# Dispatch of tokens to experts: one buffer region per expert, the first half of the tokens scattered once it is chosen

## Chip, cores and metric

The kernel runs on one core of one Trainium2 chip. The metric is the device time of one execution in microseconds (us); less is better. TensorE is called PE, VectorE DVE, ScalarE ACT, GpSimd POOL and SyncE SP.

## What is computed

The kernel computes a small transformer: x is 4 x 512 x 256 in float32. An attention with 32 query heads and 8 key heads (rotated, causal) is added to x; then a mixture of experts "f"; then a differential attention with 32 heads of 8; then a mixture of experts "h" with the same weights. Norms stand ahead of each. The experts matter here, on 2048 tokens of 256 values:

```python
scores = softmax(xt @ Wg.T)                        # 16 experts
# the best 2 of 4 groups by their largest score, then the best 4 experts of those
topi = top_k(masked, 4)[1]
weights = take_along_axis(scores, topi, axis=1)
h = silu(xt @ W1[e].T) * (xt @ W3[e].T)            # 176 wide, for each expert e
y = sum over the token's 4 experts of weight * (h @ W2[e].T)
z = silu(xt @ Ws1.T) * (xt @ Ws3.T) @ Ws2.T        # shared by all, 352 wide
return y + z
```

## The kernel before

Each engine has its program written out by hand, with semaphores between them. After an attention, `pe_ffn`, `act_seam` and `dve_seam` project its result, add it to x, normalize it into `y_sb` (16 blocks of 128 tokens, with the transposes in `xnT_all`) and compute the scores for 8 blocks at a time (`logits_ps`, half 0 and half 1).

**Choosing.** In `dve_ffn`, `scores(hf)` makes the softmax (ACT does the exponentials) and masks the groups, `choose(hf)` finds the four experts of each token (`pick`, and `taken`, 128 x 8 x 16 of ones and zeros). When both halves are chosen, PE counts (`counts`, L1886): with a triangle of ones and 16 more matmuls it finds each token's rank within its expert over all tokens, and each expert's total. `slots` (L1298) makes of the totals the first row of each expert in `x_slots`, where the experts lie one behind the other, each rounded up to a multiple of `HALF` = 64 rows; `assign(hf)` (L1314) makes the row of each token and choice, `slot_i`. Then `full_tiles`, `pair_units`, `singles`, `places` and `order` work out which rows each of the 72 tiles of 128 rows reads, and which expert it belongs to; they are spread over the steps of the shared experts.

**Shared experts.** PE does `shared_in(k)` and `shared_out(k)` for k = 0 to 11 (3 for each of 4 batches), ACT the silu, DVE the product `hw` and, at every third step, the sum into x (`add_shared`).

**Scatter.** `pool_ffn` writes the tokens into `x_slots` in DRAM, in 64 indirect DMAs (16 blocks x 4 choices, 128 rows of 265 values each): 32 after `assign(0)`, 32 after `assign(1)`. Number n waits for number n - 2, so two are in flight. After the last one come the 80 indirect DMAs that add the results of the tiles to y (`result_out`).

**Tiles.** SP's `sp_ffn_slots` waits for `e_order`, stores x of batches 0 to 2 into y (`store_x`), waits for the first 40 scatters (`EARLY_T` = 10 blocks) and then loads tile after tile from `x_slots` into a ring of 8 (`load(j)`, with the row read from `first_row` into a register), tiles from 24 on only after all 64 scatters. PE turns and multiplies them in pairs; DVE scales result j into `yt`, a ring of 8 too, so that result 8 waits until result 0 has been stored by POOL.

**Clearing.** Rows that no token fills must be zero. In the first attention SP issues after the loads of each of its slots n a clear of 512 rows of `x_slots` (19 in all, L436) and one of y (22, L441). Every fourth slot, SP then moves the maxima `mT` that PE needs (`sp_move_maxima`, L375).

```python
                if s == "a" and n < SLOT_ROWS // (4 * P):
                    sp.dma_start(x_slots[n * 4 * P:(n + 1) * 4 * P, :].rearrange("(a p) e -> p a e", p=P),
                                 zero.unsqueeze(1).to_broadcast([P, 4, EW])).then_inc(sm("cleared"), 16)
```

## Time and profile before

| | |
|---|---|
| median of 3 executions | 1373.87 us (1372.12 to 1375.77) |
| the profiled execution: its time, its span | 1371.78 us, 1370.0 us |
| busy: PE, DVE, ACT, POOL | 1147.9, 874.3, 543.2, 688.1 us |
| DMA: bytes moved, mean rate | 177.42 MB, 129 GB/s |
| mean granted clock of PE | 0.928 |
| first attention, experts f | about 105 to 345 us, 345 to 680 us |
| second attention, experts h | about 780 to 1020 us, 1020 to 1350 us |

Busy times are those in which an engine executes an instruction; a wait is not busy. In rows of the time line a row is start, duration, engine, line of the kernel, operation, out<-in, with in brackets the idle time before it and what ended it. "SPq" rows are the issues of DMAs by SP, "DMA" rows in the chain of waits the transfers themselves.

### The profile page before, as it was taken

The numbers are of one execution on the slowest core, as the hardware profiler recorded it, in microseconds if no ns is written. First come the engines' busy times: TensorE is split into PE (matmuls) and PEld (weight loads), VectorE is DVE, ScalarE is ACT, GpSimd is POOL, SyncE is SP. The second block draws the span as 40 slices with busy tenths as digits, with TensorE's granted clock in tenths as the row PEclk, the third lists the DMA queues.
The fourth block names the chain that finished last, engine by engine and source line by source line (L and its number), as shares of the span: only waits on it lengthen the run. The fifth ranks groups of instructions, "written<-read, shape, count | busy, mean of one in ns | idle before, by whom it ended". The sixth has DMA issues, their size and how long they took to land.

```text
span 1370.0 us, 25841 instructions
## 1 busy us (share of the span) xinstructions
PE 1147.9 (84%) x8690; PEld 616.4 (45%) x8690; DVE 874.3 (64%) x2061; ACT 543.2 (40%) x846; POOL 688.1 (50%) x841
## 2 busy tenths in 40 slices
PE   6888889898889479999568799999888886999990
PEld 2343334342755256665234344444346543665650
DVE  5688889891683135555288799999657722455543
ACT  2124767779421022222122377777855001222210
POOL 4452344444016558777563445555530455777671
PEclk9987999999989799999779899999999997999995
DMA  4424656520913468888664422122044136788868
GB/s 138 145 85 148 187 177 195 156 60 2 297 41 128 133 169 141 150 158 145 105 196 152 152 61 58 52 61 55 10 151 136 64 130 175 151 161 154 156 88 260
DMA packets 154353, 177.42 MB, mean 129 GB/s; under 512 B 20016, under 2 KB 139760, under 8 KB 153712
## 3 DMA queue, kind: packets, MB, share of 16 engines
q1 hardware_dynamic: 124336, 136.38, 34.0%
q0 software_dynamic: 29184, 38.36, 16.4%
q8 instruction: 73, 1.20, 0.4%
q10 hardware_dynamic: 704, 1.02, 0.2%
q14 instruction: 56, 0.46, 0.1%
HBM read 91.12 MB, written 83.78 MB: 128 GB/s over the span
## 4 chain that ended last, share of the span: by engine, by line
PE 49%; DVE 18%; DMA 16%; issue 6%; ACT 5%; SPq 3%; POOL 3%; POOLq 0%; ACTq 0%; DVEq 0%
DMA x_slots<-y_sb,slot_i 11%; PE pair_ps L1976 9%; PE o_ps L1747 8%; DVE nm L1116 4%; ACT arena L842 4%; PE pair_ps L2009 3%; DVE bm L1116 3%; PE pair_ps L2012 2%; PE t_ps L1773 2%; PE pair_ps L1697 2%; PE pair_ps L1578 2%; DMA arena<-mT 2%; PE pair_ps L1672 2%; PE pair_ps L1677 2%; PE pair_ps L1963 2%
## 5 line engine op out<-in xcount | busy, mean ns | idle before, releaser
L842 ACT ACTIVATE arena<-pair_ps 128x1024 f32<-128x1024 f32 x320 | 323.4, 1024 | 133.5 <-PE pair_ps L1672 78.2
L616 POOL TENSOR_SCALAR_AFFINE_SELECT arena<-arena 128x512 f32<-128x512 f32 (+1 forms) x320 | 175.0, 547 | 244.7 <-ACT arena L842 244.2
L1116 DVE TENSOR_REDUCE nm<-pair_ps 128x2 f32<-128x1024 f32 (+1 forms) x192 | 232.5, 1222 | 36.4 <-PE pair_ps L1721 33.2
L685 POOL DMA_INDIRECT x_slots<-y_sb,slot_i x128 | 123.0, 961 | 197.7 <-DVE slot_i L1323 114.1
L1747 PE MATMUL o_ps<-arena 128*9 128x512 f32 (+7 forms) x2048 | 177.3, 441 | 4.2 <-POOL arena L616 4.1
L1976 PE MATMUL pair_ps<-arena 128*128 x512 | 167.8, 469 | 1.8 <-ACT arena L893 1.8
L1116 DVE TENSOR_REDUCE bm<-pair_ps 128x8 f32<-128x1024 f32 x128 | 155.3, 1217 | 4.0 <-PE pair_ps L1721 1.0
L701 POOL DMA_INDIRECT y_f<-xnT,dest x80 | 125.0, 1562 | 42.8 <-DVE xnT L1466 19.3
L701 POOL DMA_INDIRECT y_h<-xnT,dest x80 | 124.6, 1558 | 43.2 <-DVE xnT L1466 20.3
L1449 DVE TENSOR_TENSOR arena<-arena,pair_ps 128x128 f32<-128x128 f32 x144 | 41.4, 288 | 116.2 <-ACT arena L898 74.3
L1976 PEld LDWEIGHTS pair_ps<-arena 128*128 128x128 f32 x512 | 94.2, 195 | 43.4 <-issue 5.9
L898 ACT ACTIVATE arena<-pair_ps 128x176 f32<-128x176 f32 x144 | 45.7, 317 | 145.2 <-PE pair_ps L1976 89.6
L1466 DVE TENSOR_SCALAR xnT<-pair_ps,slot_w 128x256 f32<-128x256 f32 x144 | 64.8, 481 | 55.4 <-PE pair_ps L2014 15.6
L1919 PE MATMUL pair_ps<-arena 128*128 128x512 f32 (+1 forms) x192 | 89.8, 614 | 0.0
L1721 PE MATMUL pair_ps<-c_b 64*128 64x128 bf16 (+1 forms) x1280 | 85.2, 211 | 0.0
L1721 PEld LDWEIGHTS pair_ps<-c_b 64*128 64x128 bf16 x1280 | 60.9, 98 | 34.0 <-issue 4.6
L1672 PE MATMUL pair_ps<-arena 51*128 51x512 bf16 x256 | 51.4, 398 | 21.4 <-DMA arena<-mT 8.5
L893 ACT ACTIVATE arena<-t_ps 128x512 f32<-128x512 f32 x36 | 21.5, 597 | 120.3 <-PE t_ps L1951 90.4
L2009 PE MATMUL pair_ps<-arena 128*128 x224 | 60.4, 393 | 9.4 <-DVE arena L1457 9.4
L1697 PE MATMUL pair_ps<-arena 48*128 48x512 bf16 x256 | 51.4, 395 | 19.2 <-ACT arena L842 14.8
L1747 PEld LDWEIGHTS o_ps<-arena 128*9 128x9 f32 (+1 forms) x2048 | 39.0, 93 | 53.2 <-issue 30.3
L889 ACT ACTIVATE sil<-pair_ps 128x512 f32<-128x512 f32 (+1 forms) x24 | 14.3, 595 | 109.8 <-PE pair_ps L1919 105.2
(273 smaller groups left out, 2019.4 us busy)
## 6 DMA issues: line engine op xcount, KB each, us to landing
arena<-x_slots SPq DMA_DIRECT2D x128, 132.5 KB
arena<-in_w SPq DMA_DIRECT2D x4, 2816.0 KB, 19.0
x_slots<-hw SPq DMA_DIRECT2D x19, 530.0 KB, 3.7
arena<-q_a SPq DMA_DIRECT2D x64, 96.0 KB
arena<-q_b SPq DMA_DIRECT2D x64, 96.0 KB
y_f<-hw SPq DMA_DIRECT2D x11, 512.0 KB, 4.2
y_h<-hw SPq DMA_DIRECT2D x11, 512.0 KB, 4.3
arena<-in_w SPq DMA_DIRECT2D x2, 2048.0 KB, 17.2
```

The source lines that it names most:

```text
L616: pool.affine_select(p, p, pattern, ALU.is_ge, 0.0, base=0, channel_multiplier=-1)\
L685: pool.indirect_dma_start(x_slots, bass.IndirectOffsetOnAxis(ap=slot_i[:, t, k:k + 1], axis=0), y_sb[:, t, :], None).then_inc(sm(scat(n)[0 ...
L701: pool.indirect_dma_start(y_acc[f][s % ACCS], bass.IndirectOffsetOnAxis(ap=dest[:, to:to + 1], axis=0), yt[:, j % XR, :], None, compute_op ...
L842: act.activation(p_ring[:, U % RING, :], pair_ps[:, pair_at("T", n, u)].rearrange("p a c -> p (a c)"), ACT.Exp, scale=SCALE).then_inc(sm(" ...
L1116: dve.tensor_reduce(dst, src, X, ALU.max, negate=not 2 <= u < 4).then_inc(sm("t_max_done"), 1)
L1672: mm = pe.matmul(ps, k_of(s, g, h, KM, 0, P), q_of(g, h, KM, 0, T), start=True, stop=True, skip_group_check=True)
L1697: pe.matmul(ps, q_of(g, h, KQ, 3 * P, T), k_of(s, g, h, KQ, 0, T), start=True, stop=False, skip_group_check=True)
L1721: mm = pe.matmul(blocks[:, :, 64 * half:64 * half + 64], mask_h[lo:lo + 64, half * P:half * P + P], ident_b[lo:lo + 64, lo:lo + 64].unsque ...
L1747: mm = pe.matmul(o_ps[32 * h:32 * h + vw, T - c:T], v_all[:, g, TB * b + j, v0:v0 + vw], p_ring[:, U % RING, a:a + c], start=j == 0, stop= ...
L1919: mm = pe.matmul(st_ps[0:m, k % 2, 512 * a:512 * a + 512], ws13[:, a, e, r:r + m], xnT_all[:, e, b * T:(b + 1) * T], start=e == 0, stop=e ...
L1976: mm = pe.matmul(s_ps[:, j % 2, 0:2 * INTER], xgT[:, j // 2 % 2, j % 2, c, :], w13[:, c, ds(e, 1), :].rearrange("p a i -> p (a i)"), start ...
L2009: pe.matmul(st_ps[:, h, 512:512 + E], hsT[:, h, :], w2[:, 0, ds(e, 1), :].rearrange("p a d -> p (a d)"), start=True, stop=False, skip_grou ...
```

## The change

`x_slots` gets one region of 2048 + 64 rows for each expert (`REGION`), and behind the 16 regions 512 empty rows; it grows from 9728 to 34304 rows. The row of a token is then 2112 times its expert plus its rank, and needs no totals. PE counts each half by itself, the first half between the two parts of `shared_in(0)`. DVE assigns the first half before it scores the second (whose maxima it takes first, so that ACT can work on them), and the later steps of the order move back by one step k. Of the clears of `x_slots` only that of the empty rows is left; in their place SP copies, for each expert, 64 empty rows behind its last token, when the totals are known (`pad_row`), ahead of the stores of x. The rest follows from the numbering: the tile's first row is made of region and place.

```diff
@@ -62,11 +62,12 @@
...
-EMPTY = NJ * P
+ROWS = NT * P
+REGION = ROWS + HALF
+EMPTY = NE * REGION
 SLOT_ROWS = EMPTY + 4 * P
...
@@ -432,8 +435,8 @@
...
-                if s == "a" and n < SLOT_ROWS // (4 * P):
-                    sp.dma_start(x_slots[n * 4 * P:(n + 1) * 4 * P, :].rearrange("(a p) e -> p a e", p=P),
+                if s == "a" and n == 0:
+                    sp.dma_start(x_slots[EMPTY:EMPTY + 4 * P, :].rearrange("(a p) e -> p a e", p=P),
                                  zero.unsqueeze(1).to_broadcast([P, 4, EW])).then_inc(sm("cleared"), 16)
...
@@ -488,11 +491,16 @@
...
+            sp.wait_ge(sm("e_pads"), 1 + past(f, 1))
+            for e in range(NE):
+                row = sp.value_load(pad_row[0:1, e:e + 1], min_val=0, max_val=EMPTY - HALF)
+                sp.dma_start(x_slots[ds(row, HALF), :], x_slots[EMPTY:EMPTY + HALF, :]).then_inc(sm("padded"), 16)
             sp.wait_ge(sm("e_order"), 1 + past(f, 1))
             for b in range(B - 1):
                 store_x(b)
-            for half in "ab":
-                sp.wait_ge(sm("scat0" + half), 16 * EARLY_T * TOPK // 2 * (1 + past(f, 1)))
+            sp.wait_ge(sm("padded"), 16 * NE * (1 + past(f, 1)))
+            for parity in range(2):
+                sp.wait_ge(sm(f"scat{parity}"), 16 * (EARLY_T * TOPK // 2 + past(f, NT * TOPK // 2)))
...
@@ -669,21 +677,12 @@
...
-            def scat(n):
...
-
             def scatter(n):
                 t, k = n // TOPK, n % TOPK
                 if n >= 2:
-                    name, value = scat(n - 2)
-                    pool.wait_ge(sm(name), value)
+                    pool.wait_ge(sm(f"scat{n % 2}"), 16 * (n // 2 + past(f, NT * TOPK // 2)))
                 pool.indirect_dma_start(x_slots, bass.IndirectOffsetOnAxis(ap=slot_i[:, t, k:k + 1], axis=0),
-                                        y_sb[:, t, :], None).then_inc(sm(scat(n)[0]), 16)
+                                        y_sb[:, t, :], None).then_inc(sm(f"scat{n % 2}"), 16)
...
@@ -712,7 +711,7 @@
...
-            pool.wait_ge(sm("cleared"), 16 * (SLOT_ROWS // (4 * P) + 22))
+            pool.wait_ge(sm("cleared"), 16 * 23)
...
@@ -1242,14 +1241,17 @@
...
-            def scores(hf):
+            def maxima(hf):
 
...
+
+            def scores(hf):
+
+                w = sc[:, hf]
                 dve.wait_ge(sm("e_sexp"), hf + 1 + past(f, 2))
...
@@ -1295,25 +1297,13 @@
...
-            def slots():
-
-
-                total = s_ps[:, 0, NT * NE:(NT + 1) * NE]
-                dve.wait_ge(sm("e_counts"), 1 + past(f, 1))
...
+                dve.wait_ge(sm("e_counts"), hf + 1 + past(f, 2))
+                ranks = s_ps[:, 0, hf * TH * NE:(hf + 1) * TH * NE].rearrange("p (t e) -> p t e", t=TH)
+                ch(dve.scalar_tensor_tensor(slot[:, half], experts_i.unsqueeze(1).to_broadcast([P, TH, NE]), float(REGION),
+                                            ranks, ALU.mult, ALU.add))
...
@@ -1328,6 +1318,16 @@
...
+                total = s_ps[:, 0, NT * NE:(NT + 1) * NE]
+                early = s_ps[:, 0, (NT + 1) * NE:(NT + 2) * NE]
+                dve.scalar_tensor_tensor(pad_row[:], experts_i, float(REGION), total, ALU.mult, ALU.add)\
+                    .then_inc(sm("e_pads"), 1)
+                ch(dve.tensor_scalar(a[:, 0, :], early, 0.5 - HALF, 1.0 / P, ALU.add, ALU.mult))
+                ch(dve.tensor_scalar(nt[:, 0, :], total, HALF / 2 - 0.5, 1.0 / HALF, ALU.add, ALU.mult))
+                rounded(nt[:, 0, :])
+                ch(dve.tensor_tensor(c, low16.rearrange("p (i j) -> p i j", i=NE),
+                                     nt[:, 0, :].unsqueeze(1).to_broadcast([P, NE, NE]), ALU.mult))
+                ch(dve.tensor_reduce(nt[:, 1, :], c, X, ALU.add))
...
@@ -1397,13 +1397,14 @@
...
+                region, row = spare[:, 0:NP], spare[:, NP:2 * NP]
+                ch(dve.tensor_scalar(tile_e[:], ps[:, NP:2 * NP], float(NE), float(NE - 1), ALU.add, ALU.min))
+                ch(dve.tensor_scalar(region, ps[:, NP:2 * NP], float(REGION), float(EMPTY), ALU.mult, ALU.add))
+                ch(dve.scalar_tensor_tensor(row, ps[:, 0:NP], float(HALF), region, ALU.mult, ALU.add))
+                ch(dve.tensor_scalar(slot_id[:], row[:, 0:NJ], lane_slot[f], None, ALU.add))
+                ch(dve.tensor_scalar(slot_id[HALF:P, MIX[0]:NJ:6], row[HALF:P, NJ:NP], lane_slot[f][HALF:P], None, ALU.add))
+                ch(dve.tensor_copy(first_row[:, 0:NJ], row[:, 0:NJ]))
+                dve.tensor_scalar(first_row[:, NJ:NP], row[:, NJ:NP], float(HALF), None, ALU.add).then_inc(sm("e_order"), 1)
...
@@ -1413,31 +1414,36 @@
...
-            scores(0)
-            choose(0)
-            scores(1)
-            choose(1)
-            for k in range(3 * B):
+            def weigh(k):
                 m = SCH[k % 3][1]
                 dve.wait_ge(sm("e_sil"), k + 1 + past(f, 3 * B))
                 dve.wait_ge(sm(f + "_hw_used"), k + 1)
                 dve.tensor_tensor(hw[0:m, k % 2, :], sil[0:m, k % 2, :], st_ps[0:m, k % 2, 512:1024], ALU.mult)\
                     .then_inc(sm(f + "_sil_free"), 1)
-                if k % 3 == 0 and k > 0:
+
+            maxima(0)
+            scores(0)
+            choose(0)
+            maxima(1)
+            assign(0)
+            weigh(0)
+            scores(1)
+            weigh(1)
+            choose(1)
+            for k in range(2, 3 * B):
+                weigh(k)
+                if k % 3 == 0:
                     add_shared(k // 3 - 1)
-                if k == 0:
-                    slots()
-                    assign(0)
-                if k == 1:
+                if k == 2:
                     assign(1)
-                if k == 2:
+                if k == 3:
                     full_tiles()
-                if k == 3:
+                if k == 4:
                     pair_units()
                     singles()
-                if k == 4:
+                if k == 5:
                     places()
-                if k == 5:
+                if k == 6:
                     order()
...
@@ -1883,16 +1889,19 @@
...
-            def counts():
-
-
-                pe.wait_ge(sm("e_taken"), 2 + past(f, 2))
...
+            def counts(hf):
+
+
+                pe.wait_ge(sm("e_taken"), hf + 1 + past(f, 2))
+                half = slice(hf * TH, hf * TH + TH)
+                pe.matmul(s_ps[:, 0, hf * TH * NE:(hf + 1) * TH * NE], upper, taken[:, half, :].rearrange("p t e -> p (t e)"),
+                          start=True, stop=False, skip_group_check=True)
+                last = NT if hf == 1 else TH - 1
+                for t in range(last):
+                    first = max(t + 1, hf * TH)
+                    n = (TH if hf == 0 else NT + 1) - first + (1 if hf == 1 and t < EARLY_T else 0)
+                    mm = pe.matmul(s_ps[:, 0, first * NE:(first + n) * NE].rearrange("p (n e) -> p n e", n=n), ones,
+                                   taken[:, t, :].unsqueeze(1).to_broadcast([P, n, NE]), start=False, stop=t == last - 1,
...
@@ -1915,6 +1924,8 @@
                 b, (r, m) = k // 3, SCH[k % 3]
                 pe.wait_ge(sm(f + "_sil_free"), k + 1)
                 for a in range(2):
+                    if k == 0 and a == 1:
+                        counts(0)
                     for e in range(CE):
                         mm = pe.matmul(st_ps[0:m, k % 2, 512 * a:512 * a + 512], ws13[:, a, e, r:r + m],
                                        xnT_all[:, e, b * T:(b + 1) * T], start=e == 0, stop=e == CE - 1)
...
@@ -1933,11 +1944,12 @@
...
-            counts()
             for k in range(3 * B):
-                if k == 3:
+                if k == 1:
+                    counts(1)
+                if k == 4:
                     scan()
```

What follows are rows of the program in each engine's order, for layer f; names in brackets are the semaphores that a row waits for. DVE before, from the choice of the second half (`taken`) to the first rows of `assign(0)`:

```order
L1289 TENSOR_REDUCE taken<-scratch 128x128 [waits straight]
L1424 TENSOR_TENSOR hw<-sil,pair_ps 128x512 [waits f_hw_used,e_sil]
L1304 TENSOR_SCALAR scratch<-pair_ps 128x16 [waits e_counts]
L1295 TENSOR_SCALAR scratch<-scratch 128x16 [waits straight]
L1296 TENSOR_SCALAR scratch<-scratch 128x16 [waits straight]
L1306 TENSOR_TENSOR arena<-c_f,scratch 128x256 [waits straight]
L1308 TENSOR_REDUCE scratch<-arena 128x16 [waits straight]
L1309 TENSOR_SCALAR scratch<-scratch 128x16 [waits straight]
L1310 TENSOR_SCALAR scratch<-pair_ps 128x16 [waits straight]
L1311 TENSOR_TENSOR scratch<-pair_ps,scratch 128x256 [waits straight]
L1318 TENSOR_TENSOR arena<-scratch 128x512 [waits straight]
L1320 TENSOR_REDUCE scratch<-arena 128x32 [waits straight]
```

and now, from the choice of the first half:

```order
L1291 TENSOR_REDUCE taken<-scratch 128x128 [waits straight]
L1248 TENSOR_REDUCE scratch<-pair_ps 128x8 [waits e_lg]
L1249 TENSOR_TENSOR scratch<-pair_ps,scratch 128x128 [waits straight]
L1305 SCALAR_TENSOR_TENSOR scratch<-c_f,pair_ps 128x128 [waits e_counts]
L1308 TENSOR_TENSOR arena<-scratch 128x512 [waits straight]
L1310 TENSOR_REDUCE scratch<-arena 128x32 [waits straight]
L1311 TENSOR_SCALAR y_sb<-scratch 128x8x4 [waits straight]
L1312 COPY y_sb<-top 128x8x4 [waits straight]
L1313 CAST slot_i<-scratch 128x32 [waits straight]
L1421 TENSOR_TENSOR hw<-sil,pair_ps 128x512 [waits f_hw_used,e_sil]
L1256 TENSOR_REDUCE scratch<-scratch 128x8 [waits e_sexp]
```

`assign(0)` (L1305 to L1313) now stands behind the first `taken`, ahead of the second softmax (L1256), and waits for counts of its own; the operations of `slots` are gone from here.

PE before, at the second part of the shared experts' input:

```order
L1919 MATMUL pair_ps<-arena 128x512 [waits f_sil_free,f_w,a_out_x]
L1919 MATMUL pair_ps<-arena 128x512 x3
L1919 MATMUL pair_ps<-arena 128x512 [waits f_sil_free]
L1919 MATMUL pair_ps<-arena 128x512 x3
L1890 MATMUL pair_ps<-taken,c_b 128x256 [waits e_taken]
L1894 MATMUL pair_ps<-taken,c_b 128x272
L1894 MATMUL pair_ps<-taken,c_b 128x256
```

and now:

```order
L1930 MATMUL pair_ps<-arena 128x512 [waits f_sil_free,f_w,a_out_x]
L1930 MATMUL pair_ps<-arena 128x512
L1897 MATMUL pair_ps<-taken,c_b 128x128 [waits e_taken]
L1903 MATMUL pair_ps<-taken,c_b 128x112
L1903 MATMUL pair_ps<-taken,c_b 128x96
L1903 MATMUL pair_ps<-taken,c_b 128x80
L1903 MATMUL pair_ps<-taken,c_b 128x64
L1903 MATMUL pair_ps<-taken,c_b 128x48
L1903 MATMUL pair_ps<-taken,c_b 128x32
L1903 MATMUL pair_ps<-taken,c_b 128x16
L1930 MATMUL pair_ps<-arena 128x512 x2
L1930 MATMUL pair_ps<-arena 128x512 [waits f_sil_free]
```

The counts of the first half (L1897, L1903) stand between the two parts of `shared_in(0)`; those of the second half come behind `shared_out(0)` and `shared_in(2)`.

SP before, at the start of the tiles:

```order
L542 DMA wo<-in_b_wo 128x2x256
L485 DMA y_f<-x_sb 128x4x256 [waits e_z_free,e_order]
L485 DMA y_f<-x_sb 128x4x256 [waits e_z_free] x2
L489 TENSOR_LOAD first_row [waits scat0b,scat0a]
L489 ISA x2
L464 ISA
L464 DMA arena<-x_slots 128x265
```

and now, from the last but one of the 16 copies on (the first waits for `e_pads`):

```order
L497 DMA x_slots<-x_slots 16x1060
L496 TENSOR_LOAD pad_row
L496 ISA x2
L497 ISA
L497 DMA x_slots<-x_slots 16x1060
L488 DMA y_f<-x_sb 128x4x256 [waits e_z_free,e_order]
L488 DMA y_f<-x_sb 128x4x256 [waits e_z_free] x2
L492 TENSOR_LOAD first_row [waits scat1,scat0,padded]
L492 ISA x2
L467 ISA
L467 DMA arena<-x_slots 128x265
```

Each copy takes a read of `pad_row` into a register and a DMA from DRAM to DRAM; all stand ahead of the stores of x and the wait for `e_order`.

## Rows read from the trace of the kernel before

**Rows 1.** The page, part 4: lines of the chain that ended last.

```profile
DMA x_slots<-y_sb,slot_i 11%; PE pair_ps L1976 9%; PE o_ps L1747 8%; DVE nm L1116 4%; ACT arena L842 4%; PE pair_ps L2009 3%; DVE bm L1116 3%; PE pair_ps L2012 2%; PE t_ps L1773 2%; PE pair_ps L1697 2%; PE pair_ps L1578 2%; DMA arena<-mT 2%; PE pair_ps L1672 2%; PE pair_ps L1677 2%; PE pair_ps L1963 2%
```

**Rows 2.** Time line of POOL (start us, us, what, [idle before <-releaser]).

```profile
401.64 1.17 POOL L685 DMA_INDIRECT x_slots<-y_sb,slot_i  x1 [58.20 <-DVE slot_i L1323]
...
406.00 0.96 POOL L685 DMA_INDIRECT x_slots<-y_sb,slot_i  x1 [1.90 <-DMA x_slots<-y_sb,slot_i]
...
422.50 0.96 POOL L685 DMA_INDIRECT x_slots<-y_sb,slot_i  x1 [0.30 <-issue]
...
424.31 0.96 POOL L685 DMA_INDIRECT x_slots<-y_sb,slot_i  x1 [0.84 <-DMA x_slots<-y_sb,slot_i]
...
435.51 0.96 POOL L685 DMA_INDIRECT x_slots<-y_sb,slot_i  x1 [0.52 <-DMA x_slots<-y_sb,slot_i]
...
506.72 0.96 POOL L685 DMA_INDIRECT x_slots<-y_sb,slot_i  x1 [1.63 <-DMA x_slots<-y_sb,slot_i]
...
1072.08 1.05 POOL L685 DMA_INDIRECT x_slots<-y_sb,slot_i  x1 [55.90 <-DVE slot_i L1323]
...
1171.74 0.96 POOL L685 DMA_INDIRECT x_slots<-y_sb,slot_i  x1 [0.37 <-issue]
```

**Rows 3.** Time line of PE, seams of f and h.

```profile
383.02 9.05 PE L1919 MATMUL pair_ps<-arena 128*128 128x512 f32 x16
...
395.53 0.28 PE L1890 MATMUL pair_ps<-taken,c_b 128*128 128x256 bf16 x1 [3.46 <-DVE taken L1289]
...
395.65 1.19 PE L1894 MATMUL pair_ps<-taken,c_b 128*128 128x272 bf16 x16
...
469.64 0.66 PE L1951 MATMUL t_ps<-c_f,arena 128*128 128x128 f32 x2 [16.15 <-DMA arena<-x_slots]
...
1138.42 0.66 PE L1951 MATMUL t_ps<-c_f,arena 128*128 128x128 f32 x2 [14.45 <-DMA arena<-x_slots]
```

**Rows 4.** Time lines of DVE (f) and PE (h), waits in the tiles.

```profile
512.07 0.48 DVE L1466 TENSOR_SCALAR xnT<-pair_ps,slot_w 128x256 f32<-128x256 f32 x1 [8.13 <-DMA y_f<-xnT,dest]
...
1180.81 1.13 PE L2009 MATMUL pair_ps<-arena 128*128 x4 [2.35 <-DVE arena L1457]
```

**Rows 5.** Time line of DVE, seams of f and h.

```profile
385.68 1.01 DVE L1289 TENSOR_REDUCE taken<-scratch 128x128 bf16<-128x512 f32 x1
...
386.91 0.29 DVE L1251 TENSOR_TENSOR scratch<-pair_ps,scratch 128x128 f32<-128x128 f32 x1
...
399.29 0.69 DVE L1318 TENSOR_TENSOR arena<-scratch 128x512 f32<-128x512 f32 x1
...
401.17 0.18 DVE L1323 CAST slot_i<-scratch 128x32 int32<-128x32 f32 x1
...
410.10 0.74 DVE L1412 TENSOR_TENSOR x_sb<-x_sb,o_ps 128x256 f32<-128x256 f32 x2
...
1055.66 1.01 DVE L1289 TENSOR_REDUCE taken<-scratch 128x128 bf16<-128x512 f32 x1
```

**Rows 6.** Time line of SP, its DMA issues before the tiles of f.

```profile
424.72 18.56 SPq L485 DMA_DIRECT2D y_f<-x_sb  x3
...
467.37 1.67 SPq L464 DMA_DIRECT2D arena<-x_slots  x2
```

**Rows 7.** Chain of waits in time (start us, us, what), first attention and f.

```profile
108.87 2.69 DMA arena<-mT
...
136.92 1.06 SPq L436
...
139.64 3.72 DMA arena<-mT
...
418.41 2.34 DMA x_slots<-y_sb,slot_i
```

**Rows 8.** Time line of PE, first attention.

```profile
111.60 0.61 PE L1672 MATMUL pair_ps<-arena 51*128 51x512 bf16 x2 [1.72 <-DMA arena<-mT]
```

**Rows 9.** Waits on PE, 105 to 345 us (total us, times, longest).

```profile
PE pair_ps L1672 <- DMA arena<-mT: 8.1, 6, 1.7
```

55 lines of the change are left out of this document (14 added, 41 removed).

## The prediction

> **What bounds the kernel now.** I read the page first, then the time line of GpSimd (POOL) around the two expert stages, then VectorE (DVE), TensorE (PE) and SyncE (SP) there, and last the chain of waits in the first attention.
>
> In the chain that ended last the scatters of tokens (`x_slots<-y_sb,slot_i`) have the largest share, 11% of 1370 us [rows 1]; the other large parts are matmuls. In the "f" layer the 64 scatters start at 401.64, the last at 506.72; in "h" at 1072.08 and 1171.74 [rows 2]. With two in flight, undisturbed, 12 steps take 406.00 to 422.50, 1.375 us each; while the stores of x run, 6 steps take 424.31 to 435.51, 1.87 us each [rows 2]. Over all 63 steps the mean is 105.08/63 = 1.67 us in f and 99.66/63 = 1.58 in h.
>
> Who waits for them? PE finishes the shared experts at 453.5 and begins the first tile at 469.64, after 16.15 us of idleness that a load from `x_slots` ended [rows 3]; in h the same idleness is 14.45 us [rows 3]. Those loads wait for scatter 40 of 64. Then DVE stands still 8.13 us before result 8, since a buffer of results comes free only when POOL, behind scatter 64, stores result 0; its first result goes out right behind the last scatter's 506.72 [rows 2, 4]. In h PE waits 2.35 us at that place [rows 4]. So both gates of the expert stage hang on the scatters, which run from the first one in a queue of their own. If the whole queue starts earlier by some time, both gates open earlier by it, and everything behind moves.
>
> What starts it? DVE's second table of places. The choice of the first half is finished at 385.68 + 1.01 = 386.69, but DVE then scores and chooses the second half, PE counts all tokens, and `slots` and `assign(0)` end at 401.35 [rows 5]. PE stood still 3.46 us before these counts, which took 1.19 us [rows 3].
>
> **The first scatter.** After the change DVE needs only: `maxima(1)`, two instructions at about 0.3 us, as now until 386.91 + 0.29 = 387.20 [rows 5]; beside it `counts(0)` on PE, whose `taken` is there at 386.7 and whose 8 matmuls take 8/17 of 1.31 us (395.53 to the end of the second group, 396.84) = 0.6 us, so until 387.4 with the hand-over [rows 3]; then one new instruction from PSUM on 128x128, for which I take 0.33 us from the 0.29 us of L1251 of the same size and its gap, and the old `assign` of 399.29 to 401.35, 2.06 us [rows 5]. That is 387.4 + 0.33 + 2.06 = 389.8, and POOL follows 0.3 us behind as before: 390.1. Gain in f: 401.6 - 390.1 = 11.5 us. In h `taken` of the first half ends at 1055.66 + 1.01 = 1056.67 [rows 5]; plus 3.4 gives 1060.1 against 1072.08: 12.0 us. PE is between two groups of the shared experts then (383.02 + 9.05 = 392.07 is the end of the second [rows 3]) and waits some 1.5 us, where it waited 3.46 later; the counts of the second half come 1 us sooner than PE gets round to them. I put the shared stage's end down as unmoved. If I am wrong by 4 us there it still ends before the first load, since the idleness of 16.15 and 14.45 us is longer than the shift.
>
> **The pads.** They are 16 copies per layer, 64 rows x 1060 B = 67.8 KB each, half of a scatter's 135.7 KB, 1.09 MB in all. No copy from DRAM to DRAM is in the trace. The nearest rows: the first two stores of x, 1.05 MB, are beside the six slow steps, which took 11.20 us instead of 8.25, so 2.95 us more [rows 2, 6]; that gives 3.1 us by bytes. The pads come in 16 pieces over some 21 us (two loads with a row read from a register span 1.67 us with their issue, so about 1.3 us for each [rows 6]), which leaves the scatters room: I take 2 us per layer. Bounds: 0, and, if a copy displaces half a scatter's step, 16 x 0.69 = 11 us. For SP they cost 21 us: from about 411 (`e_pads` comes in DVE's step 3, after it has added the first batch's shared part, now until 410.10 + 0.74 [rows 5]) to 432. Behind them in SP's queue are the stores of x; the third of them was issued at 424.72 + 18.56 = 443.3 at the earliest anyway [rows 6], as it waits for the shared experts. `e_order` moves one step back, to about 431, also before it. Scatter 40 lands at about 457, so SP has some 13 us to spare. The seven small operations that come from `slots` into `full_tiles` (some 1.9 us on DVE) and two or three more in `order` lie in the same slack: cost 0, covered by SP's wait for scatter 40; without cover they would be about 3 us.
>
> **The first attention.** 18 of the 19 clears of `x_slots` (530 KB) go, the 22 clears of y stay. At five places the clear stands in SP's queue right before the maxima, `mT`, that PE needs, as at 136.92: the clear's issue 1.06 us, then that of a clear of y, then the transfer of mT, 3.72 us [rows 7]. Before the first clear the same transfer took 2.69 us [rows 7]. The waits of PE for mT are 8.1 us in six [rows 9]; the first of them, 1.72 us, has no clear before it [rows 8], so 6.4 us are to be had. An issue of some 0.43 us (more where the queue backs up) and up to 1 us of transfer go at each. Low bound 5 x 0.43 = 2.2 us, high bound 6.4; I take 4.5, since the transfer's excess is due to two clears and one remains.
>
> **The sum.** f: -11.5 + 2 = -9.5; h: -12.0 + 2 = -10.0; attention -4.5; together -24.0 us. The profiled execution took 1371.8 us, so 1347.8; the median shown, 1373.9, is 2.1 above it, and against it the forecast is **1350 us**.
>
> **A rule against it.** The regions lie 2112 rows x 1060 B = 2.24 MB apart and all of them span 36 MB, where the old slots spanned 10 MB. In the trace every scatter already goes to rows all over its 10 MB and lands in 2.34 us [rows 7]. The Trainium skill, "DMA: Bandwidth & Descriptors", section "Latency and other measured facts", tells of copies whose HBM row pitch is a large power of two: 2 MiB gave 164 instead of some 214 GB/s, and a few KiB of padding restored it. By that rule 2.24 MB is a padded 2 MiB, and the sum would stay; if the regions did alias, it would give the rival below. No run here shows it yet.
>
> **Rivals.**
> - **The gate for the first tiles doesn't move.** If SP's pads and order end later than scatter 40 (21 us of issue turn out 35 or more), PE starts at 469.6 as before, and only the second gate moves: about -7 in f (8.13 of [rows 4], less what DVE would not have needed) and -2.4 in h, with attention -14: 1360. For it: SP's new row of 16 register reads. Against: 13 us of slack. Chance 0.08.
> - **The pads are dear.** At 11 us per layer nearly the whole shift is eaten: -0.5 - 1.0 - 4.5 = -6: 1368. For it: one queue of copies DRAM to DRAM, never seen here. Against: the stores moved as many bytes for 3 us. Chance 0.1.
> - **Slower: the scatters themselves slow down** because their targets lie apart. Their 126 steps take 204.7 us now. From a clean step of 1.375 + 24.0/126 = 1.57 us on, nothing is left; at the contended 1.87 us throughout it would be +0.5 x 126 = +62, less 24: 1412. Against: rows are written singly, and the descriptor's 1060 B are unchanged. Chance 0.05.
> - **The first scatters don't start**: if POOL is still held (the clears, a later count), only attention gains: 1369 to 1372, no change that can be told. Chance 0.05, since neither engine has other work there.
>
> **Numbers.** The forecast case has 0.72. Its own range: pads 0 and attention 6.4 give -29.9, 1344; pads 5 each and attention 2.2 give -15.7, 1358. With the executions' own spread of 2 us and the first rival on both sides I give 1341 to 1364; what is left out is about 0.2. A measurement can tell about 0.3%, 4 us, from no change: faster 0.90 (the forecast, the first rival, and the dear pads), same 0.05, slower 0.05.
>
> **What would show it.** In the changed profile: the first scatter some 3.6 us after the first `taken` (it was 15.0); the clean step still 1.375 us; pads landing beside scatters with steps under 1.6 us; PE's idleness before the first tile 6 to 8 us instead of 16; the stall before result 8 still there at about its old length; PE's waits for mT down from 8.1 to 2 to 4 us. Wrong it would be if the clean step is longer, if SP issues the first load later than scatter 40 lands, or if the shared experts end later than the first load.

## The result, and the profile after

The change makes the kernel faster: 1354.74 us against 1374.24, medians of four runs each; ratio 0.9845, 95% interval 0.9817 to 0.9873, so 17.5 to 25.1 us less. The forecast was 1350 (1341 to 1364), 24 us less; the medians differ by 19.5. All times given here are medians of a kernel's fast executions: one slower execution each of the repeated kernel, of the wide regions and of the four in flight behind scatter 40 (1.5% or more above that kernel's fastest) is left out. The profiled execution took 1352.4 us with a span of 1350.7 (before 1370.0), clock 0.932 (0.928). The changed kernel's own runs spread over 9.4 us, the kernel before's over 3.7.

The page of the profile of the changed kernel, part 4, shares of the engines in the chain that ended last; the x scatters' DMA has 10% of the span there, where it had 11% [rows 1]:

```profile
PE 53%; DVE 17%; DMA 13%; issue 6%; ACT 6%; POOL 3%; SPq 2%; POOLq 0%; ACTq 0%; DVEq 0%
```

The time line of GpSimd (POOL) in the changed kernel: scatters (L684) and results (L700).

```profile
385.20 1.17 POOL L684 DMA_INDIRECT x_slots<-y_sb,slot_i  x1 [44.66 <-DVE slot_i L1313]
...
448.89 0.96 POOL L684 DMA_INDIRECT x_slots<-y_sb,slot_i  x1 [0.33 <-DMA x_slots<-y_sb,slot_i]
...
489.36 0.96 POOL L684 DMA_INDIRECT x_slots<-y_sb,slot_i  x1 [0.67 <-DMA x_slots<-y_sb,slot_i]
490.63 1.62 POOL L700 DMA_INDIRECT y_f<-xnT,dest  x1 [0.30 <-issue]
...
657.25 1.56 POOL L700 DMA_INDIRECT y_f<-xnT,dest  x1 [0.31 <-issue]
...
1044.62 1.06 POOL L684 DMA_INDIRECT x_slots<-y_sb,slot_i  x1 [45.22 <-DVE slot_i L1313]
...
1152.44 0.96 POOL L684 DMA_INDIRECT x_slots<-y_sb,slot_i  x1 [0.95 <-DMA x_slots<-y_sb,slot_i]
...
1319.86 1.56 POOL L700 DMA_INDIRECT y_h<-xnT,dest  x1 [0.30 <-issue]
```

Against [rows 2] the first scatter of f is 16.4 us earlier and the last 17.4; in h the first is 27.5 earlier, the last 19.3. The first scatter follows the first half's choice closely now, as the time line of DVE shows:

```profile
380.98 1.00 DVE L1291 TENSOR_REDUCE taken<-scratch 128x128 bf16<-128x512 f32 x1
...
382.52 0.29 DVE L1305 SCALAR_TENSOR_TENSOR scratch<-c_f,pair_ps 128x128 f32<-128x128 f32 x1
...
384.73 0.18 DVE L1313 CAST slot_i<-scratch 128x32 int32<-128x32 f32 x1
```

A gate is a point that PE can't pass before some scatter is done. There are two in each layer: the first tile, whose load waits for scatter 40, and the ninth tile, which needs a buffer that POOL frees by storing result 0, and it does that behind scatter 64. The time line of PE at the first tile (L1963) and at the ninth (L2021), f and h, answering to [rows 3, 4]:

```profile
455.60 0.66 PE L1963 MATMUL t_ps<-c_f,arena 128*128 128x128 f32 x2 [9.99 <-DMA arena<-x_slots]
...
497.60 1.64 PE L2021 MATMUL pair_ps<-arena 128*128 x3 [2.72 <-issue]
...
1115.82 0.66 PE L1963 MATMUL t_ps<-c_f,arena 128*128 128x128 f32 x2 [10.71 <-DMA arena<-x_slots]
...
1160.65 1.64 PE L2021 MATMUL pair_ps<-arena 128*128 x3 [6.89 <-DVE arena L1463]
```

SP's issues in f (16 copies of zero rows, three stores of x, the first load), answering to [rows 6], and PE's waits for mT at 105 to 345 us, answering to [rows 9]:

```profile
404.76 21.56 SPq L497 DMA_DIRECT2D x_slots<-x_slots  x16
426.42 8.97 SPq L488 DMA_DIRECT2D y_f<-x_sb  x3
452.75 1.74 SPq L467 DMA_DIRECT2D arena<-x_slots  x2
```

```profile
PE pair_ps L1678 <- DMA arena<-mT: 2.5, 2, 1.7
```

Where the 19.3 us of span came from: the first attention ends 4.6 us sooner (`maxima(0)` starts at 372.11 where it was 376.68); f gives 17.4 by its last scatter and 16.6 by its last result (657.25 for 673.85); between there and h's first maxima (1031.54 for 1046.80) 1.3 us are lost, in work that the change doesn't touch; h gives 12.2 at its first scatter and loses 8.2 of it along the scatters (107.8 us for 63 steps, before 99.7).

### The profile page after: what moved, and what is told of

It is laid out like the page before. It is cut to its first block, busy times and chain, and to the rows that moved or that the text cites. A ratio compares the mean times of both kernels' runs of the same rounds, so it can differ in the third digit from the quotient of the medians.

```text
span 1350.7 us, 26055 instructions
## 1 busy us (share of the span) xinstructions
PE 1148.2 (85%) x8706; PEld 615.5 (46%) x8706; DVE 873.9 (65%) x2067; ACT 542.6 (40%) x846; POOL 690.0 (51%) x841
## 4 chain that ended last, share of the span: by engine, by line
PE 53%; DVE 17%; DMA 13%; issue 6%; ACT 6%; POOL 3%; SPq 2%; POOLq 0%; ACTq 0%; DVEq 0%
PE pair_ps L1988 10%; DMA x_slots<-y_sb,slot_i 10%; PE o_ps L1753 9%; ACT arena L841 4%; DVE nm L1115 4%; PE pair_ps L2021 4%; DVE bm L1115 3%; PE pair_ps L2024 2%; PE t_ps L1779 2%; PE pair_ps L1703 2%; PE pair_ps L1683 2%; PE pair_ps L1584 2%; PE pair_ps L1708 2%; PE pair_ps L1995 2%; PE pair_ps L1678 2%
## 5 line engine op out<-in xcount | busy, mean ns | idle before, releaser
L684 POOL DMA_INDIRECT x_slots<-y_sb,slot_i x128 | 123.8, 968 | 179.9 <-DVE slot_i L1313 89.9
L1988 PE MATMUL pair_ps<-arena 128*128 x512 | 171.6, 477 | 1.8 <-ACT arena L892 1.0
L700 POOL DMA_INDIRECT y_f<-xnT,dest x80 | 125.0, 1563 | 43.5 <-DVE xnT L1472 17.7
L700 POOL DMA_INDIRECT y_h<-xnT,dest x80 | 124.7, 1559 | 43.3 <-issue 21.6
L1988 PEld LDWEIGHTS pair_ps<-arena 128*128 128x128 f32 x512 | 95.8, 199 | 44.6 <-issue 8.0
L2021 PE MATMUL pair_ps<-arena 128*128 x224 | 61.2, 397 | 9.6 <-DVE arena L1463 6.9
L892 ACT ACTIVATE arena<-t_ps 128x512 f32<-128x512 f32 x36 | 21.5, 597 | 108.3 <-PE t_ps L1963 78.5
L2021 PEld LDWEIGHTS pair_ps<-arena 128*128 128x128 f32 x224 | 42.1, 194 | 30.6 <-issue 19.4
```

The lines of the kernel that those rows point to most:

```text
L684: pool.indirect_dma_start(x_slots, bass.IndirectOffsetOnAxis(ap=slot_i[:, t, k:k + 1], axis=0), y_sb[:, t, :], None).then_inc(sm(f"scat{n ...
L700: pool.indirect_dma_start(y_acc[f][s % ACCS], bass.IndirectOffsetOnAxis(ap=dest[:, to:to + 1], axis=0), yt[:, j % XR, :], None, compute_op ...
L1988: mm = pe.matmul(s_ps[:, j % 2, 0:2 * INTER], xgT[:, j // 2 % 2, j % 2, c, :], w13[:, c, ds(e, 1), :].rearrange("p a i -> p (a i)"), start ...
L2021: pe.matmul(st_ps[:, h, 512:512 + E], hsT[:, h, :], w2[:, 0, ds(e, 1), :].rearrange("p a d -> p (a d)"), start=True, stop=False, skip_grou ...
```

## The experiments

All kernels start from the changed one unless said otherwise. Each ratio is to the kernel before of the same batch; the kernels of a batch ran on one chip one after another. There were three batches. The first, on chip 3, had the start held back, the clears put back, the copies twice and the four in flight. The second, on chip 13, had the copies doubled in f, the compact regions and the two kernels with four in flight and a late start. The third, on chip 3 again, had the changed kernel repeated, the wide regions and the two with four in flight in one part. Edits are shown by their main lines; `...` marks lines left out, mostly counts of semaphores that follow from the rest.

**The early start held back.** GpSimd waits for both halves of the slot table:

```diff
-            pool.wait_ge(sm("e_slots"), 1 + past(f, 2))
+            pool.wait_ge(sm("e_slots"), 2 + past(f, 2))
```

> The changed kernel, with one wait raised: GpSimd issues its first scatter only when the second half's slots are written, too. Regions, zero rows, clears, PE's and DVE's order stay. In the changed kernel's trace the two slot tables are written 13.0 us apart in f (384.73 and 397.74) and 13.4 us apart in h (1044.16 and 1057.53). Theory (the time is set by the end of scatter 40, so what counts is how early the scatters start): the first tile of both layers moves back by about 12 us, a little less than 13 where scatters escape the zero rows' copies (21 us long); the time grows by 22 to 26 us, to about 1379, back to that of the kernel before. Rival (the gain is the shorter shared stage and the fewer clears, the scatters had slack): the time grows by 0 to 5 us, to at most 1360.

Measured: 1374.51 us, 0.9982 to 1.0030 of the kernel before, so 20 us more than the changed kernel, 22 by the ratios. The first scatters are at 397.76 and 1069.77, and PE's idleness before the first tiles is longer than before the change (16.15 and 14.45), as its shared experts end earlier:

```profile
465.19 0.66 PE L1963 MATMUL t_ps<-c_f,arena 128*128 128x128 f32 x2 [19.54 <-DMA arena<-x_slots]
...
1136.51 0.66 PE L1963 MATMUL t_ps<-c_f,arena 128*128 128x128 f32 x2 [18.77 <-DMA arena<-x_slots]
```

With the first scatter's time undone, nothing of the change is left in the total, though the fewer clears are still there (`maxima(0)` starts at 371.97): what they give, the rest of the added work takes back.

**The clears put back:**

```diff
+                if s == "a" and 0 < n < 19:
+                    sp.dma_start(x_slots[n * 4 * P:(n + 1) * 4 * P, :].rearrange("(a p) e -> p a e", p=P),
+                                 zero.unsqueeze(1).to_broadcast([P, 4, EW])).then_inc(sm("cleared"), 16)
...
```

> The changed kernel, with the 18 clears of 512 rows put back into the first attention; they zero rows that the scatters and zero-row copies write later anyway. Everything behind the first attention stays. Theory (the fewer clears gave 4.6 us in the first attention and nothing elsewhere): mT waits on PE return to about 8 us, the first maxima from 372.1 to 376.7, and the time grows by 4 to 5 us, to about 1359.5. Rival (the rest of the 19.5 us, or most of it, came from them, for example since DMA rings are emptier later): over 8 us. Rival (the attention's change is a difference between two profiles and not of the clears): within 1.5 us of the changed kernel.

Measured: 1356.55 us, ratio 0.9848 to 0.9918. The medians say 1.8 us more than the changed kernel, the ratios 5.2, and the interval overlaps the changed kernel's (0.9817 to 0.9873), so the time alone tells nothing. The trace is clearer: PE waits for mT again,

```profile
PE pair_ps L1681 <- DMA arena<-mT: 8.9, 6, 2.3
```

and `maxima(0)` starts at 380.54. In the three profiles of this study with 19 clears it starts at 376.68, 378.75 and 380.54, in the eleven with one clear between 371.97 and 376.99, means 378.7 and 374.4: 4.3 us, about as expected, and the attention alone scatters by 2 us or more either way.

**Zero rows copied twice**, the second copy into a tensor that nobody reads:

```diff
                 sp.dma_start(x_slots[ds(row, HALF), :], x_slots[EMPTY:EMPTY + HALF, :]).then_inc(sm("padded"), 16)
+                sp.dma_start(spill[e * HALF:(e + 1) * HALF, :], x_slots[EMPTY:EMPTY + HALF, :]).then_inc(sm("padded"), 16)
...
```

> The changed kernel, with each of the 16 copies of 64 zero rows issued a second time, into a tensor that nobody reads; twice the issues and twice the bytes. SP's issues last 21.6 us in f now and would last about 43, to 447, and the three stores of x that follow (9 us) would end at about 457 where scatter 40 lets the first load go at 452.8: so the queue itself is worth about 4 us per layer here, 8 in all. Theory (the copies also slow the scatters beside them, from 1.375 to 1.57 us a step): some 13 more steps of 0.2 us are hidden behind that longer queue in part, the scatter steps between 425 and 447 stay near 1.57, the time grows by 8 to 12 us. Rival (the copies cost nothing beyond SP's time, the slower steps are the wider spread of the targets): steps beside the second half of the copies are no longer than without them (1.40), and the time grows by 8 us or less. Rival (copies dear, 11 us a layer): 20 us or more.

Measured: 1359.34 us, ratio 0.9856 to 0.9925, 4.6 us more than the changed kernel by medians and 6.2 by ratios; the intervals overlap slightly. The first tile comes 69.4 us behind the first scatter, where the changed kernel has 70.4. A further copy costs SP only some 0.6 us of issue; the read of the row's register was the larger part of the 1.35 us. So SP's issues in f last 31.3 us and not the 43 expected, and its queue doesn't become a gate. In the time line of SP:

```profile
411.81 0.55 SPq L498 DMA_DIRECT2D x_slots<-x_slots  x1
412.40 0.59 SPq L499 DMA_DIRECT2D spill<-x_slots  x1
413.75 0.54 SPq L498 DMA_DIRECT2D x_slots<-x_slots  x1
```

The scatters take 106.8 us in f and 108.3 in h, against 104.2 and 107.8 in the changed kernel's first profile and 102.4 and 105.2 on average over four profiles with the copies once (the changed kernel's two, clears back, and wide). So doubling 1.09 MB costs some 0.5 to 4.4 us a layer, no better told than that, since the four lie up to 4.4 us apart; 11 us a layer is ruled out.

**Copies doubled in f, none in h:**

```diff
-            for e in range(NE):
-                row = sp.value_load(pad_row[0:1, e:e + 1], min_val=0, max_val=EMPTY - HALF)
-                sp.dma_start(x_slots[ds(row, HALF), :], x_slots[EMPTY:EMPTY + HALF, :]).then_inc(sm("padded"), 16)
+            for e in range(NE if f == "f" else 0):
+                row = sp.value_load(pad_row[0:1, e:e + 1], min_val=0, max_val=EMPTY - P)
+                sp.dma_start(x_slots[ds(row, P), :], x_slots[EMPTY:EMPTY + P, :]).then_inc(sm("padded"), 16)
```

> The changed kernel, with the copies of zero rows made twice as long in f (128 rows each, the same 16 issues) and left out in h, so that the rows behind the tokens there hold zeros or tokens of f: the zeroing of h's tiles is left out. One run so shows both. Theory (the copies' packets slow the scatters beside them a little): in h the steps 16 to 23 fall from 1.6 to about 1.45, the scatters as a whole get 3 to 5 us shorter, SP reaches the stores 22 us earlier; f's steps beside the copies grow from 1.6 to about 1.75 and f gets 2 to 4 us longer; the time within 3 us of the changed kernel. Rival (copies cost nothing beside scatters): both layers stay within 1.5 us of the changed kernel's, apart from where the stores fall. Rival (the copies are what gives back 8 us in h): h 8 us shorter.

Measured: 1353.70 us, ratio 0.9838 to 0.9893, no difference from the changed kernel. The 63 steps take 103.3 us in f and 102.8 in h. So h's copies explain some 2 to 5 us of its 8: in the five profiles with copies in h, the early start and regions of the full size (the changed kernel's two, clears back, copies twice, and wide) h's scatters took 103.4 to 108.3 us, mean 105.8, and here 102.8. The first profile lay at the long end. With the start held back, and the same copies beside them, they took 101.3. For the kernel before there is one profile with two in flight, and how far its 99.7 would move from one to the next isn't known.

**Distance of the regions**, one line each, shorter for this input alone, and four times as long:

```diff
-REGION = ROWS + HALF
+REGION = 11 * HALF
```

```diff
-REGION = ROWS + HALF
+REGION = 4 * (ROWS + HALF)
```

> The changed kernel, with a region of 704 rows for each expert in place of 2112, so that the 16 regions lie 0.75 MB apart and not 2.24 MB (this input fills at most 584 rows of one). It differs from the change in the distances alone; for other inputs it would overflow. Theory (distance costs nothing; steps of 1.27 us are issue-bound and the longer ones wait for the scatter two before): steps, first tile and time stay within 3 us of the changed kernel, about 1355. Rival (targets far apart slow each scatter: the 1.57 us beside the copies and the 1.68 us of the first eight come from it): steps fall by 0.1 to 0.2 us, first tiles come 4 to 8 us earlier, the time falls by 8 to 16 us.

> The changed kernel, with regions four times as long: 8448 rows, 8.96 MB apart, in place of 2112 and 2.24 MB. Right for every input; only distances change. Theory (distance costs nothing): 1350 to 1358, within 4 us of the changed kernel of this call. Rival (rows far apart cost the scatters, as the 3 to 5 us fewer in either layer with regions 0.75 MB apart suggest): scatters take 108 us or more in both layers and the time grows by 5 us or more.

> The changed kernel itself, once more, beside the next three on the same chip: its nine and more other runs spread over 9.4 us, and the run with the compact regions stood 8 us below its median while the two intervals overlap. Theory (distance of regions costs nothing): median 1350 to 1358, the same as the compact and the wide one to 4 us; steps of the first forty scatters 1.55 to 1.65 on average in either layer, by chance. Rival (distance costs): this one's 64 scatters take 103 to 108 us again where the compact one took 100 and 101.

Measured: compact 1346.38 us, 0.9808 to 0.9858; wide 1352.97, 0.9834 to 0.9925; the changed kernel again, beside the wide one, 1353.40, 0.9833 to 0.9913. Wide and changed are equal: four times the distance costs nothing that can be told (both were disturbed in f, as told below). The compact one has the shortest scatters of those with two in flight and an early start (100.0 and 101.3 us), but its interval overlaps the changed kernel's first one, and it ran in another batch than the wide. Whether 0.75 MB gains a few us over 2.24 stays open. The steps at their best speak against it: with regions 2.24 MB apart and no copies in h, the best eight steps there took 1.36 us each, as before the change, and with 0.75 MB 1.39 and 1.41.

**Four scatters in flight.** A scatter waits for the fourth before it:

```diff
-                if n >= 2:
-                    pool.wait_ge(sm(f"scat{n % 2}"), 16 * (n // 2 + past(f, NT * TOPK // 2)))
+                if n >= 4:
+                    pool.wait_ge(sm(f"scat{n % 4}"), 16 * (n // 4 + past(f, NT * TOPK // 4)))
...
```

> The changed kernel, with four x scatters in flight in place of two: scatter n waits for n - 4 (four semaphores; two are freed by letting the last stores and one constant's load count on others). Of the 63 steps of f in the changed kernel 19 were issue-bound at 1.27 us, the others waited for the scatter two before, up to 3.8 us. Theory (the step is set by the landing of the scatter two before, and the slow steps beside the copies, stores and tile loads are that latency): steps fall to 1.27 to 1.35 us, scatter 40 is issued 10 to 12 us earlier, the first tile comes up to 10 us earlier in f and in h (PE is idle 10.0 and 10.7 us before it), and the time falls by 10 to 20 us, to 1335 to 1345. Rival (what limits a scatter is the DMA engines' or the memory's rate for scattered rows, so more in flight only queue up): steps stay at 1.55 to 1.7 on average and the time stays within 3 us.

Measured: **1315.83 us** (1313.50 to 1318.07, five runs), ratio 0.9543 to 0.9614; 39 us less than the changed kernel (37 by the ratios), about twice the most that was expected. GpSimd's time line has one pace now:

```profile
436.91 0.96 POOL L684 DMA_INDIRECT x_slots<-y_sb,slot_i  x1 [0.30 <-issue]
...
467.70 0.96 POOL L684 DMA_INDIRECT x_slots<-y_sb,slot_i  x1 [0.30 <-issue]
468.96 1.62 POOL L700 DMA_INDIRECT y_f<-xnT,dest  x1 [0.30 <-issue]
...
642.88 1.56 POOL L700 DMA_INDIRECT y_f<-xnT,dest  x1 [0.30 <-issue]
```

0.96 us busy and 0.30 us of issue, 1.27 us a step nearly throughout, beside copies, stores and tile loads alike: 80.8 us for f's 63 steps, where two in flight took 104.2. Rows could go out at this rate all along; the steps of 1.4 to 3.8 us were mostly waits for the scatter two before. (The 19 steps that the expectation calls issue-bound are those for which the trace names no releaser; only 11 of f's 63 were shorter than 1.30 us.) Where the traces of the kernels with four in flight give a scatter's way from issue to landing, it took 2.4 to 5.4 us, 2.6 to 2.8 in the median. My estimate from this: 2.7/1.27, so little more than two, are under way on average, and the third and fourth are there for those that land late. Three in flight was not run. From the first scatter to the last result f takes 256.0 us (272.1 with two in flight) and h 253.6 (275.2), 37.7 us less together. PE's first tile starts right behind the shared experts and the ninth tile waits for nothing:

```profile
1094.33 0.63 PE L1963 MATMUL t_ps<-c_f,arena 128*128 128x128 f32 x4 [1.81 <-issue]
```

**The same in the kernel before**, and with the early start held back (the edits of this and of the first experiment together):

> The kernel before, with four x scatters in flight in place of two and nothing else changed. Theory (in both kernels the steps above 1.27 us wait for the landing of the scatter two before, whatever else is in the DMA engines): steps 1.27 to 1.30 us here too, the last scatter 24 us earlier in f (506.7 to 482) and 19 us in h, PE's waits before the first tile and before tile 8 shrink from 16.2 and 7.1 us (f) to about 5 and 0 to 2, time 1332 to 1342. The changed kernel with four in flight stands at 1315.8, so what the change brings would be 16 to 26 us with four in flight, as with two. Rival (four in flight pays only against the copies of zero rows): time 1360 or more.

> The changed kernel with four x scatters in flight, and GpSimd's first scatter held until the second half's slots are written, 13 us later. Theory (with two in flight and with four, PE waits for scatter 40 and, at the ninth tile, for the results, which start behind scatter 64): scatter 40 issued at about 449 in f, first tile at 455 to 457 where it now starts at 451.05 behind the shared experts, results from 482 and not 469, a wait of 3 to 7 us at the ninth tile; 8 to 12 us a layer, the time grows by 16 to 24 us over 1315.8, to 1332 to 1340. Rival (with four in flight the early start is worth nothing any more, since PE had no wait left): 1316 to 1322.

Measured: 1340.42 us (0.9750 to 0.9797) and 1338.90 us (0.9749 to 0.9799), steps of 1.27 us in both. So four in flight is worth 31 us to the kernel before (its median in that batch was 1371.55) and 39 to the changed one, and the early start is worth 23 us with four in flight (27 by the ratios), 20 with two (22 by the ratios). The two add.

**Four in flight in one part only**, behind scatter 40 (shown) or up to it (2 and 4 exchanged):

```diff
...
+                back = 4 if n >= EARLY_T * TOPK else 2
+                if n >= back:
+                    m = n - back
+                    pool.wait_ge(sm(f"scat{m % 4}"), 16 * (m // 4 + 1 + past(f, NT * TOPK // 4)))
...
```

> The changed kernel, with two scatters in flight up to scatter 40 and four after it. The first gate (scatter 40, first tile) stays, the last scatter and the first result come 24 x (1.65 - 1.27) = 9 us earlier. Theory (the last scatter sets the end, through the results that start behind it and the ninth tile that waits for the first of them): the ninth tile's waits of 2.7 us in f and 6.9 us in h go, and the time falls by those 9 to 10 us, to 1343 to 1347. Rival (only the first gate counts): within 2 us of the changed kernel. Rival (the last scatter sets the end all the way): it falls by 18 us or more.

> The changed kernel, with four scatters in flight up to scatter 40 and two after it. Scatter 40 comes 12 to 14 us earlier in both layers, and the last scatter and the results come earlier by as much. Theory (both gates move, PE is held by the shared experts' end first and by the results after): first tile at about 451 without a wait for loads, the ninth tile still waits, 3 to 7 us, since the last 24 scatters take 1.7 us each beside the tile loads; the time falls by 20 to 28 us, to 1327 to 1335, and the rest to the 1315.8 of four throughout is the late gate's. Rival (only the last scatter counts, and its 12 us each): it falls by 24 us in any case and the two halves of the change add up to 39 with e11_late_four's 15.

Measured: 1389.16 us (1.0130 to 1.0224) and 1444.49 us (1.0512 to 1.0595), slower than the kernel before, against every theory. Both ran in the batch of the wide and the repeated kernel. Their scatters did as expected (in the early one 1.29 us a step on average up to scatter 40, 1.62 at most), but the other engines stood still beside them. The time line of all engines of the early one:

```profile
442.15 0.96 POOL L686 DMA_INDIRECT x_slots<-y_sb,slot_i  x1 [0.30 <-issue]
442.71 0.18 DVE L1343 TENSOR_TENSOR scratch<-scratch 128x16 f32<-128x16 f32 x1 [1.23 <-DVE scratch L1300]
443.63 0.95 POOL L686 DMA_INDIRECT x_slots<-y_sb,slot_i  x1 [0.51 <-DMA x_slots<-y_sb,slot_i]
444.28 0.28 DVE L1344 TENSOR_SCALAR scratch<-scratch,c_f 128x16 f32<-128x16 f32 x1 [1.39 <-DVE scratch L1343]
444.99 0.96 POOL L686 DMA_INDIRECT x_slots<-y_sb,slot_i  x1 [0.41 <-issue]
445.69 0.24 DVE L1345 TENSOR_SCALAR scratch<-scratch,c_f 128x16 f32<-128x16 f32 x1 [1.13 <-DVE scratch L1344]
```

DVE does one small operation for each scatter, where its chained operations otherwise follow each other in 0.2 us. SP's 16 copies took 52 us:

```profile
437.76 52.01 SPq L497 DMA_DIRECT2D x_slots<-x_slots  x16
```

It is not chance from one execution to the next: the six lie between 1442 and 1457 us, and from the first scatter to the first tile it takes 127 us in f and in h alike (64 and 63 with four in flight throughout). And it is bound to the scatters: behind them, from the first tile to the last result, f takes 190.5 us, no more than elsewhere. The waits that the edit changes are not the cause up to scatter 40, since until there this kernel and the one with four in flight throughout issue the same work behind the same waits; yet at the slots of f's second half DVE already waited 5.30 us here and 0.58 there:

```profile
402.60 0.29 DVE L1307 SCALAR_TENSOR_TENSOR scratch<-c_f,pair_ps 128x128 f32<-128x128 f32 x1 [5.30 <-remote]
```

```profile
398.64 0.29 DVE L1305 SCALAR_TENSOR_TENSOR scratch<-c_f,pair_ps 128x128 f32<-128x128 f32 x1 [0.58 <-PE pair_ps L1903]
```

The changed kernel shows a weaker form of it in the same batch: in f its copies took 35.5 us (21.6 in its first profile) and its shared experts ended at 467.4, where its first load was issued at 458.8. So does the wide one, with 32.8 us and 463.9. The kernel before stayed at 1372.40. The chip isn't the difference, by its number: the first batch, which shows nothing of it, ran on chip 3 too. What is, and whether four in flight throughout would have suffered there as well, is open. These two runs tell nothing of the two gates. 1315.8 rests on one batch; that four in flight gives steps of 1.27 us and some 30 us of time was seen in two.

What that disturbed profile of the changed kernel does tell, at least for f, is which gate decides. PE and POOL:

```profile
469.24 0.63 PE L1963 MATMUL t_ps<-c_f,arena 128*128 128x128 f32 x4 [1.81 <-issue]
```

```profile
488.80 0.96 POOL L684 DMA_INDIRECT x_slots<-y_sb,slot_i  x1 [0.30 <-issue]
490.07 1.62 POOL L700 DMA_INDIRECT y_f<-xnT,dest  x1 [0.31 <-issue]
...
661.03 1.56 POOL L700 DMA_INDIRECT y_f<-xnT,dest  x1 [0.31 <-issue]
```

The first tile is 13.6 us later than in the first profile, the last scatter 0.6 earlier, the last result only 3.8 later; with the wide regions the first tile is 10.1 us later, the last scatter 1.0 and the last result 1.1. Read over the profiles of f, the last result comes at the later of two sums, to some 2 us: the last scatter plus 167 us (before 167.1, changed 167.9, held 167.8), or the first tile plus 192 us, which is PE without a gap (four in flight 191.8, here 191.8, wide 192.6). The changed kernel: 489.4 + 168 = 657, or 455.6 + 192 = 647; its last result is at 657.25. With four in flight: 467.7 + 167 = 635, or 451.05 + 192 = 643; it is at 642.88. In h the same two sums (167, and 191) give the last result to some 2 us as well. In the two kernels with four in flight and a late start, where the two sums are nearly equal, it comes 4 and 5 us above the later one (656.05 and 657.20; in h 4 and 5 too), and the two of this batch with four in flight in one part are left aside. So this is a rule read from profiles and fitted to them; no undisturbed run moved one gate alone.

## Why the prediction was right, and where not

The forecast was right, in its range and in what brings the time. Three of its terms came out as worked; one was too small by 6 us, and another, too large by 3, hid half of that by luck.

- **The first scatter: right.** Forecast 3.4 to 3.6 us from the end of `taken` to the scatter; measured 381.98 to 385.20, 3.2, in h 1041.41 to 1044.62, 3.2. Net of the attention the start moved by 11.9 us in f (forecast 11.5), and net of all before it by 12.2 in h (12.0). Holding it back took the whole gain away, and with four in flight too it cost 23 us.
- **The first attention: right.** Waits for mT 8.1 to 2.5 us (forecast 2 to 4), seam 4.6 us earlier (4.5). Over fourteen profiles, 19 clears against one are worth 4.3.
- **The pads: right in size in f up to the first gate, hidden behind it.** The first 40 scatters of f took 1.7 us more than before (63.7 for 62.0), the last 24 2.6 less (40.5 for 43.1), so all of them 0.9 less where 2 more were forecast. Why the last 24 were faster isn't shown; over four profiles with the early start f's scatters lie between 100.2 and 104.2 us. The steps beside them were 1.57 us on average (13 steps from 404.32 to 424.78), under the 1.6 forecast. SP issued them from 404.8 and not 411.
- **h: the term that was mis-sized.** The sum had -12.0 + 2 for h's scatters. Measured at the last scatter it was -12.2 + 8.2 (5.1 of it up to scatter 40). Over five profiles the loss is nearer 6, against the one profile of the kernel before; some 3 of it vanish without the copies; the rest is not explained. By the two profiles the account is -24.0, +6.2 (h's scatters, 8.2 for the 2), +2.1 (0.8 between f's last scatter and its last result, 1.3 from there to h's first maxima), -2.9 (f's scatters, -0.9 for the 2), -0.6 (the small differences of the three first terms) = -19.2, where the spans differ by 19.3.
- **"The shared stage's end put down as unmoved": wrong, harmless.** It ended 3.3 us earlier than the attention's gain explains (445.61 for 453.49), 3.6 in h. It does so with the start held back, too (445.66), so it comes from the new order of work on DVE and PE and not from the scatters. That is why PE was idle 10.0 us and not 6 to 8: 16.15 - 11.5 + 2 = 6.65, plus 3.3. As foreseen, the shift was smaller than the idleness, so it bought nothing.
- **"Both gates open earlier by it": right in sign, and incomplete.** Both moved (first tile 14.0 and 22.6 us, last scatter 17.4 and 19.3), but by the sums above only the last scatter set the end. The first tile could have come some 9 us later in f at next to no cost (647 for 657); with the wide regions it came 10.1 later, and the last result 1.1. The forecast that the stall at the ninth tile keeps its length failed with it: it is what is left between the gates, 2.7 us in f (7.1 before) and 6.9 in h (2.4 before).
- **The rivals.** "The gate for the first tiles doesn't move" was priced at 1360 with SP's issues 35 us long. In the repeated run they were 35.5 us long in f, and the first tile of f came at 469.2, though the shared experts held it and not SP (their end was at 467.4, the first load was issued at 458.8); in h it moved. The time was 1353.4. For f the rival gave 7 us behind the attention; the last result came 12.8 us earlier there, 11.4 without the attention's 1.4. So its condition came true for one layer, by another way, and its price was too high for that layer, which fits a second gate that decides. "Pads dear", at 11 us a layer, fell with twice the copies for 5 to 6 us in all. "Targets apart" fell with regions 8.96 MB apart at 1353.0. Its sign, a longer clean step, is hardly there: the best eight steps are 1.40 us each in f and 1.42 in h, against 1.36 and 1.38 before, and 1.36 in h without the copies. The Trainium skill's rule on HBM row pitch ("DMA: Bandwidth & Descriptors", "Latency and other measured facts") was read as leaving the sum alone for 2.24 MB. The runs don't speak against it, and at 8.96 MB too the time didn't move; but the page's figures are for tiles copied with one fixed row pitch, and the rows of a scatter have none, so they can't confirm it either.

## What to carry to other kernels

Where a stage has two gates on one queue, ask for each what the end would be if it alone were left (here the last scatter + 167, the first tile + 192) before pricing a shift; in f the gate with the longer visible idleness (10.0 us against 2.7) was not the one that decided. And before moving the start of a queue of small transfers, look at its steps: where they vary between 1.27 and 3.8 us and most are released by the transfer two before, the number in flight can be the larger lever. Here it was, and the two added. A result from one batch, however tight its five runs, should be seen in a second one: here one and the same part of the program ran undisturbed in one batch and at half its speed in another.

## What was not expected of the hardware

Scattered rows of 1060 B, 128 to a scatter, go out every 1.27 us with four in flight beside all that the DMA engines carried here (share up to 0.75, 231 GB/s at 460 to 470 us), while each takes 2.3 us or more to land. And in one batch small chained operations of DVE fell to one for each scatter, 1.4 to 1.6 us apart, and started some 0.6 us into GpSimd's instruction of 0.96. The Trainium skill, "SBUF — State Buffer", section "Who interferes with whom", says that GpSimd and DVE, when DVE is in a two-port mode or has two SBUF inputs while GpSimd reads SBUF, lock each other out of a shared port pair for a whole instruction, and that PE and ACT wait for nobody. Here DVE's operations start within GpSimd's, ACT once waited 39.7 us for something that the profile calls only "remote", and SP's copies took 52 us and not 21, so that rule alone doesn't give the pattern. No run here shows what does.
